# Edge sums of a graph attention layer: one-hot blocks made four at a time on VectorE, five of eight heads scaled on ScalarE, eight row slots

## The reference

```python
p = jnp.exp(s - m[src])                                      # one weight per edge and head
denom = jax.ops.segment_sum(p, src, num_segments=n)
alpha = p / jnp.where(denom[src] == 0, 1.0, denom[src])
agg = jax.ops.segment_sum(alpha[:, :, None] * v[dst], src, num_segments=n)
att = agg.reshape(n, C) @ Wo.T + bo
```

## Time and profile before

| | |
|---|---|
| time of the kernel | 6714.76 us median of 3 runs (6714.2 to 6720.42) |
| span of the profiled execution | 6560.1 us |
| median less span (launch and end, outside the trace) | 154.7 us |
| first gather to end of the last add of `attend` | 849.3 to 1169.6 us |
| share of `attend` in the span | 4.9% |
| longest phase, the LSTM (L1654 and others) | from about 1170 us to about 5660 us |

### The profile page before, as it was taken

The page is one execution under the profiler, slowest core; times in us unless marked ns, Lnnn a source line. Parts: engine busy times, 40 slices in busy tenths (PEclk is TensorE's granted clock), DMA queues, the critical chain, the costliest instruction groups (busy, mean ns, idle before and its releaser), DMA issues. The chain is left out here.

```text
span 6560.1 us, 407056 instructions
## 1 busy us (share of the span) xinstructions
PE 5245.2 (80%) x179105; PEld 3616.3 (55%) x179105; DVE 3804.3 (58%) x22336; ACT 1879.1 (29%) x8915; POOL 677.8 (10%) x716
## 2 busy tenths in 40 slices
PE   1989757789777888777887778987777777888999
PEld 1433334566555666556665556665555555554445
DVE  7337857466666666666666666666666666574111
ACT  1210069333333333333333333333333333200100
POOL 0744345000000000000000000000000000252000
PEclk8999979899999999999999999999999999998999
DMA  2235455101000000000000000100000000221110
GB/s 90 77 92 141 117 160 162 59 28 30 1 0 0 17 28 17 0 0 8 27 27 0 0 0 22 30 9 0 0 0 0 0 0 0 77 80 56 68 36 13
DMA packets 172012, 241.50 MB, mean 37 GB/s; under 512 B 90362, under 2 KB 130938, under 8 KB 167827
## 3 DMA queue, kind: packets, MB, share of 16 engines
q0 software_dynamic: 41952, 116.33, 6.5%
q1 hardware_dynamic: 129714, 120.73, 6.0%
HBM read 224.38 MB, written 12.61 MB: 36 GB/s over the span
## 5 line engine op out<-in xcount | busy, mean ns | idle before, releaser
L1654 PE MATMUL l_bank<-l_w,l_hp 128*32 128x128 f16 x160000 | 2486.7, 220 | 823.4 <-DVE l_hp L1942 801.0
L1654 PEld LDWEIGHTS l_bank<-l_w,l_hp 128*32 128x32 f16 x160000 | 2255.6, 97 | 1431.7 <-DVE l_hp L1942 1391.2
L1906 DVE STREAM_TRANSPOSE agg<-l_bank 128x128 f32<-128x128 f32 x2500 | 792.9, 317 | 1176.6 <-PE l_bank L1654 1005.9
L1782 ACT ACTIVATE l_th<-l_z 128x8 f32<-128x8 f32 x2500 | 523.7, 209 | 2153.2 <-DVE l_z L1912 2153.2
L1664 PE MATMUL l_spare<-l_w 128*2 128x512 f16 x12120 | 865.0, 379 | 3.7 <-issue 3.7
L2128 POOL DMA_INDIRECT ga_rows<-r_table,dst_t x176 | 166.9, 948 | 4633.8 <-DMA r_table<-c_r 4508.2
L1787 ACT ACTIVATE l_tc<-l_th 128x2 f32<-128x2 f32 x2500 | 490.5, 196 | 465.5 <-DVE l_th L1929 465.5
L1918 DVE SCALAR_TENSOR_TENSOR l_terms<-l_th 128x4 f32<-128x4 f32 x2500 | 357.0, 143 | 256.7 <-ACT l_th L1782 256.7
L1936 DVE TENSOR_TENSOR l_hp<-l_go,l_tc 128x2 f16<-128x2 f32 x2500 | 422.0, 169 | 132.0 <-ACT l_tc L1787 0.9
L1912 DVE TENSOR_REDUCE l_z<-agg 128x8 f32<-128x24 f32 x2500 | 447.5, 179 | 42.6
L1942 DVE TENSOR_TENSOR l_hp<-l_full,l_hp 128x2 f16<-128x2 f32 x2500 | 422.6, 169 | 43.9 <-DVE l_full L1937 0.6
(11 more groups left out here) (428 smaller groups left out, 4913.8 us busy)
## 6 DMA issues: line engine op xcount, KB each, us to landing
w<-in_g_W SPq DMA_DIRECT2D x128, 128.0 KB, 2.1
w<-in_l_Wx SPq DMA_DIRECT2D x128, 128.0 KB, 2.1
keys<-in_src_by_tile SPq DMA_DIRECT2D x7, 1344.0 KB, 6.8
e_w<-in_e_W SPq DMA_DIRECT2D x2, 4096.0 KB
e_chosen<-chosen SPq DMA_DIRECT2D x24, 256.0 KB, 6.2
wh<-in_l_Wh SPq DMA_DIRECT2D x1, 4096.0 KB, 18.8
late<-in_l_Wh SPq DMA_DIRECT2D x1, 4096.0 KB, 19.0
late<-in_l_Wx SPq DMA_DIRECT2D x1, 4096.0 KB
```

Source lines behind the costliest of these rows:

```text
L1654: mm = pe.matmul(banks[par][q][32 * j:32 * j + 32, 0:128], hp[:, par, k, 30 - 30 * v:62 - 30 * v], w16[:, half, k, j, 256 * q + 128 * v:25 ...
L1782: act.activation(th[:, 2 * q:2 * q + 2, 1:], z[:, q, :].rearrange("p (j m) -> p j m", m=GATES), ACT.Tanh, scale=2.0 ** -Z_BITS).then_inc(s ...
L1906: dve.transpose(turn[:, par, q, :, 1:33], banks[par][q][:, 0:128].rearrange("p (m r) -> p m r", r=32)).then_inc(s_turned[q], 1)
```

## The change

R becomes 8. ON_DVE becomes 3, so VectorE scales heads 0 to 2 (192 elements) and ScalarE five heads. The one-hots of four tiles (AT_ONCE) are made by one comparison of VectorE over 512 elements. There are two such buffers of four. ScalarE makes none. The value load of add(t - 1) moves ahead of scale(t + 1), so it stands directly behind add(t - 2). TensorE sums the weights first and the rows second, and waits for a one-hot buffer only every fourth tile. The accumulator is cleared behind the first comparison, and ScalarE no longer waits for it.

```diff
-    R = 4
-    ON_DVE = 5
+    R = 8
+    ON_DVE = 3
+    AT_ONCE = 4
...
-        onehot, apart = sb("onehot", [P, R, P]), sb("apart", [P, R, P])
-        minus_lo, one = sb("minus_lo", [P, ST]), sb("one", [P, 1])
+        onehot = sb("onehot", [P, 2, AT_ONCE, P])
...
         @block.scalar
         def _(act):
-            act.wait_ge(cleared, 1)
-
-            def mark(t):
-                if t >= R:
-                    act.wait_ge(summed, t - R + 1)
-                act.activation(apart[:, t % R, :], g.numbers_f[:, :], ACT.Square,
-                               bias=minus_lo[:, t:t + 1]).then_inc(squared, 1)
-                act.wait_ge(squared, t + 1)
-                act.activation(onehot[:, t % R, :], apart[:, t % R, :], ACT.Relu, scale=-1.0, bias=one[:, :])
-
-            mark(0)
             for t in range(ST):
-                if t + 1 < ST:
-                    mark(t + 1)
                 i = t % R
...
         @block.vector
         def _(dve):
-            g.link(dve, dve.memset(acc[:, :], 0.0))
-            dve.memset(one[:, :], 1.0)
-            dve.tensor_scalar(minus_lo[:, :], lo[:, :], -1.0, None, ALU.mult).then_inc(cleared, 1)
+            def mark(u):
+                if u >= 2:
+                    dve.wait_ge(summed, AT_ONCE * (u - 1))
+                dve.tensor_tensor(onehot[:, u % 2, :, :], g.numbers_f[:, :].unsqueeze(1).broadcast_to([P, AT_ONCE, P]),
+                                  lo[:, AT_ONCE * u:AT_ONCE * (u + 1)].unsqueeze(2).broadcast_to([P, AT_ONCE, P]),
+                                  ALU.is_equal).then_inc(equal, 1)
...
-            def add(t):
-                node = dve.value_load(tile_node[0:1, t:t + 1], min_val=0, max_val=RT - 1)
+            def node_of(t):
+                return dve.value_load(tile_node[0:1, t:t + 1], min_val=0, max_val=RT - 1)
+
+            def add(t, node):
                 dve.wait_ge(summed, t + 1)
...
+            mark(0)
+            dve.memset(acc[:, :], 0.0).then_inc(cleared, 1)
             scale(0)
             for t in range(ST):
+                node = node_of(t - 1) if t >= 1 else None
                 if t + 1 < ST:
                     scale(t + 1)
+                if t % AT_ONCE == 1 and t + AT_ONCE < ST:
+                    mark(t // AT_ONCE + 1)
                 if t >= 1:
-                    add(t - 1)
-            add(ST - 1)
+                    add(t - 1, node)
+            add(ST - 1, node_of(ST - 1))
...
+                if t % AT_ONCE == 0:
+                    pe.wait_ge(equal, t // AT_ONCE + 1)
                 pe.wait_ge(scaled, t + 1)
-                pe.wait_ge(marked, t + 1)
+                pe.wait_ge(other, t + 1)
                 if t >= 4:
                     pe.wait_ge(added, t - 3)
-                pe.matmul(banks[t % 4][:, 0:C], onehot[:, i, :], rows[:, i, :], start=True, stop=True)
-                pe.matmul(banks[t % 4][:, C:W], onehot[:, i, :], weight[:, t, :], start=True,
-                          stop=True).then_inc(summed, 1)
+                mark = onehot[:, t // AT_ONCE % 2, t % AT_ONCE, :]
+                pe.matmul(banks[t % 4][:, C:W], mark, weight[:, t, :], start=True, stop=True)
+                pe.matmul(banks[t % 4][:, 0:C], mark, rows[:, i, :], start=True, stop=True).then_inc(summed, 1)
```

More of the change, by code:

```diff
@@ L1241, in attend @@
         rows = sb("rows", [P, R, C])
-        onehot, apart = sb("onehot", [P, R, P]), sb("apart", [P, R, P])
-        minus_lo, one = sb("minus_lo", [P, ST]), sb("one", [P, 1])
+        onehot = sb("onehot", [P, 2, AT_ONCE, P])
         banks = [s0.enter_context(nc.psum_tensor(f"at_bank{i}", [P, 1024], F32)) for i in range(4)]
-        passed, cleared, scaled, marked, squared = (sem("passed"), sem("cleared"), sem("scaled"), sem("marked"),
-                                                    sem("squared"))
+        passed, cleared, scaled, equal, other = sem("passed"), sem("cleared"), sem("scaled"), sem("equal"), sem("other")
         summed, added = sem("summed"), sem("added")
@@ L1294, in _ @@
                                          scale=weight[:, t, h:h + 1])
-                ins.then_inc(marked, 1)
+                ins.then_inc(other, 1)
         @block.vector
         def _(dve):
-            g.link(dve, dve.memset(acc[:, :], 0.0))
-            dve.memset(one[:, :], 1.0)
-            dve.tensor_scalar(minus_lo[:, :], lo[:, :], -1.0, None, ALU.mult).then_inc(cleared, 1)
+            def mark(u):
[4 more added lines that the diff above has]
+                                  ALU.is_equal).then_inc(equal, 1)
             def scale(t):
@@ L1316, in add @@
                     dve.wait_ge(added, t)
+                else:
+                    dve.wait_ge(cleared, 1)
                 at = acc[:, bass.ds(node * W, W)]
                 dve.tensor_tensor(at, at, banks[t % 4][:, 0:W], ALU.add).then_inc(added, 1)
+            mark(0)
+            dve.memset(acc[:, :], 0.0).then_inc(cleared, 1)
             scale(0)
             for t in range(ST):
+                node = node_of(t - 1) if t >= 1 else None
                 if t + 1 < ST:
                     scale(t + 1)
+                if t % AT_ONCE == 1 and t + AT_ONCE < ST:
+                    mark(t // AT_ONCE + 1)
                 if t >= 1:
-                    add(t - 1)
-            add(ST - 1)
+                    add(t - 1, node)
+            add(ST - 1, node_of(ST - 1))
         @block.tensor
```

## The result

The changed kernel takes 6685.66 us (median of 4 runs), the kernel before 6717.24 us in the same comparison: a ratio of 0.9952 (95% interval 0.9940 to 0.9964). It is faster by 31.6 us, where 67 were forecast. The predicted 6648 us was 38 us too low. The time lies inside the stated range of 6631 to 6689 us, but the gain is less than half of the forecast one.

The account below looks back on a forecast made before the run. The loop through four slots, 6.48 us or 1.62 a tile, was taken as the bound of `attend`. Gains of 61 (steady part) + 5 (head) - 0.5 + 1.5 (ends) = 67 us gave 6648 us, range 6631 to 6689.

Parts of the forecast that it names:

- the pace: Steady part of `attend`: GpSimd sets 1.27 us a tile, before 1.665; 155 tiles gain 61 us.
- The median is 154.7 us longer than the span of before: Whole kernel: this difference lies around the span and is kept, so the forecast is 6714.8 - 67 = 6648 us.
- The one at 1.44 us a tile: Rival, steady part of `attend`: VectorE sets the pace, 40 us gained, 6675 us; chance 0.17.
- Eight slots: Slot loop of `attend`: at most 0.87 us a tile in place of 1.62, so no longer the bound.
- GpSimd 1.25: Steady part of `attend`: a gather of 0.945 us plus 0.30 between gathers, 1.25 us a tile; the slowest engine.
- VectorE and the block number: VectorE in `attend`: 1.1 to 1.24 us a tile; the block number's load, covered by an add, costs 0 to 0.1.
- load exposed: Rival, VectorE in `attend`: value load waits for the add, 1.65 to 1.75 us a tile, 6710 to 6722 us; chance 0.05.
- GpSimd held off by VectorE: Rival, gathers of `attend`: descriptor building stalls during VectorE's two-operand reads, 1.79 us a tile, 6728 us; chance 0.05.
- DMA keeps the pace: Rival, gathers of `attend`: more in flight only land later, 1.6 us a tile, 10 us gained, 6705 us; chance 0.05.
- Head: Start of `attend` while matrices load: gathers' DMA share fixed, four more tiles fetched early, 5 us gained.
- other 8 us: Head of `attend`: further gain if the gathers' DMA share grew with the number waiting, six more gathers landing.
- Ends: Start and end of `attend`: -0.5 us at the first scaling, +1.5 from last gather to end, 8.8 us becoming 7.

Follow-up runs that it names:

- b0: The kernel before, unchanged, profiled again on a slow chip: 6708.0 us.
- a1: The changed kernel with four slots in place of eight, on a slow chip: 6746.6 us, ratio 1.0049 to the kernel before.
- a2: The changed kernel with the two products in their old order, rows first, on a slow chip: 6680.7 us, ratio 0.9949 to the kernel before.
- a6: The changed kernel with six slots in place of eight, on a quick chip: 6498.9 us, ratio 0.9922 to the kernel before.
- d1: The changed kernel, unchanged, run again on a quick chip: 6491.3 us, ratio 0.9898 to the kernel before.
- e1: The changed kernel without the small product (sums of the weights) from the fifth tile on, on a slow chip: 6696.2 us, one run.

## Why the prediction was wrong, step by step

**The step that failed** is the pace: "GpSimd is the slowest and waits for nobody while slots are free, so its pace is the stage's". Where the two kernels were timed, the pace was 1.52 us and not 1.27. GpSimd and VectorE wait there for sums that are reported late, a wait that the prediction had put at nothing (its own words for it are "hardly any wait of GpSimd for TensorE"). From the thirty-first to the last gather the kernel before takes 241.3 us there (b0) and the changed kernel 222.4. So the term of 61 us for the steady part measured 19.

**The step that hid it** is "The median is 154.7 us longer than the span of before, for what lies around it, and I keep that". In the runs of this record 1.7 to 3.4 us lie around a span. The other 150 us said that the profiled execution and the timed runs were not in the same condition, and that the page did not show the machine on which the change would be timed. It could have been doubted: no row spoke for 155 us of launch, and three timed runs within 6.2 us of each other stood against one span far from all of them. With it the rows were those of a quick chip. In their own condition they did forecast well: 6493 us of span, where the quick chip has 6487.8.

**What that cost.** On slow chips something holds the engines up where a gather would come more often than about every 1.5 us beside full work. The kernel before, at 1.665, lay just above this floor; its `attend` is 318.2 us there and 320.3 on the quick sort. The changed kernel reaches the floor and loses 0.25 us a tile to it: 145 x 0.25 = 36 us, which is the gain that went missing. That the rest came to 31.6 us is owed to the head: it gave 15 us (69.7 to 54.3 us from the first to the thirty-first gather), where 5 were counted. No rival had this mechanism. The one at 1.44 us a tile came closest to the time, 6675 us, but gave the wrong reason: the adds wait for late sums, not VectorE's work, and VectorE is busy 117.00 of 160 us.

**Eight slots** (6.96 / 8 = 0.87 us): the loop ceases to be the bound, right. The loop measured in a1 makes it 7.25 / 8 = 0.91. On slow chips this edit alone brings all of the gain. What the rest is worth on a quick chip, where eight slots with ScalarE's 1.44 us should give less than the 68.5, was not measured.

**GpSimd 1.25**: right. Gathers at 1070.60, 1071.85 and 1073.19 are 1.25 and 1.34 us apart, with 0.30 "issue" ahead, and on the quick chip the stretch has 126 at 1.27, the forecast number. Its waits for TensorE there are 23.7 us in 34 over the whole phase, 8.1 us in 25 of them in the stretch.

**ScalarE 1.20**: right, 627 scalings in 160 us at 0.24 us, 153.19 busy; it is nearly full on the quick chip.

**VectorE and the block number**: right. This is VectorE between two late sums in the changed kernel:

```profile
1069.25 0.69 DVE L1311 TENSOR_TENSOR agg<-agg,at_bank 128x520 f32 x1
1069.86 0.35 DVE L1298 TENSOR_TENSOR at_rows<-at_rows,weight_t 128x192 f32<-128x192 f32 x1
1070.15 0.70 DVE L1311 TENSOR_TENSOR agg<-agg,at_bank 128x520 f32 x1
```

Add to add is 0.90 us, with 0.17 for the comparison 1.07, and 0.29 from scaling to add: the load is covered (the rival "load exposed" wanted 1.65). The scaling takes 0.36 as worked out, the comparison 0.68.

**TensorE 1.08**: right (1071.69 to 1072.77); the order of the products is worth nothing (a2).

**GpSimd held off by VectorE**: wrong. The gather takes 946 ns at the median, 944 before, with comparison and scaling beside it.

**DMA keeps the pace**: wrong on quick chips, where the share is 0.72 (0.75 was forecast) at 1.27.

**Head**: mis-sized. 5 us were counted. On the quick chip the tiles from the thirtieth on give 145 x (1.665 - 1.28) = 56 us and the phase 72.1, so about 16 us come from what is ahead of them and behind them (17 in the head, -1 at the end). The DMA queues (packets, MB, share of 16 engines) in the 20 us that begin 5 us after the first gather, of the kernel before and of the changed kernel:

```profile
q1 hardware_dynamic: 17023, 3.13, 84.4%
q0 software_dynamic: 491, 1.62, 34.3%
```

```profile
q0 software_dynamic: 1186, 3.89, 70.4%
q1 hardware_dynamic: 16816, 0.54, 48.4%
```

The gathers' share doubled while the same 17,000 small packets of the weights went by: there their share was not fixed, it rose with the gathers waiting, and the big loads came later. The prediction had read its fixed share from a later stretch, 870 to 890 us, in which the matrices load. The changed kernel has this in the like stretch, 875 to 895 us, in which some 3000 of the small packets are still to come:

```profile
q1 hardware_dynamic: 3154, 5.53, 72.7%
q0 software_dynamic: 677, 2.21, 32.1%
...
at_rows<-v_table,dst_t POOLq DMA_INDIRECT x10, 14.0
```

The gathers' share rose there only from 23.9% to 32.1%, and they land after 14.0 us in place of 7.3. With six slots (a6) it is 18.0%. So in that stretch more gathers in flight mostly land later, about as the prediction said. It leaned on the Trainium skill, DMA: Bandwidth & Descriptors, section "Queues, rings and completion order", by which each engine goes round between its queues by packet. The measurements agree with its conclusion, in the main, while the matrices load, and not while the weights do. What parts the two stretches was not tested. For the sum, the "other 8 us" of the text were the better choice.

**Ends**: forecast +1.5 us, measured -0.7 on the quick chip. From the last gather to the end it is 9.5 us (1092.9 to 1102.4), where 7 were forecast and 8.8 were before.

**Sum.** 56 + 16 = 72 in the profiles and 68.5 in the medians, against 67 forecast. On a quick chip the total came out right with a steady part 5 us too large and a head and ends some 10 too small. That the errors cancel is luck.

## What to carry to other kernels

Hold the profiled execution against the timed runs before anything else: when the time less the span is far more than the few microseconds that lie around a span, the profile was taken in other conditions, and a phase that the change does not touch says in which. Where a chip of another sort may run the kernel, compare only runs of one chip, and repeat an edit that looks like a gain on the other sort before it is believed. Eight slots alone brought all of the gain on the slow chips. On a quick chip they were never run alone, so what the moved work adds there is not shown; the move of the heads by itself added nothing that shows in the times.

## What the runs showed of the hardware

Chips (or the conditions that they are in) differ by more than this change moves. In the scatter phase TensorE is held up on slow chips as long as GpSimd issues its scatters (the last at 385.0 us). These are stretches of the kernel before on a slow chip, during the scatters and after them:

```profile
275.00:385.00 110.00, 23.86 (x33) 8.90 (x32) 12.10 (x6) 2.71 (x5) 83.92 (x84) 0.61 0.04 4
395.00:480.00 85.00, 77.87 (x187) 36.72 (x188) 0.00 (x0) 20.27 (x31) 0.00 (x0) 0.92 0.11 37
```

33 matmuls in 110 us, then 187 in 85, all of one line, and gaps such as this one, which the trace explains by nothing but "issue":

```profile
295.73 5.08 PE L724 MATMUL st_bank<-st_wq,xn 128*128 128x512 f32 x8 [19.96 <-issue]
```

So in two phases the same holds: GpSimd's indirect transfers beside dense work of TensorE are free on quick chips and cost time on slow chips, some 150 us in one and 36 us in the other. It is not the bandwidth of the DMA engines, of which the scatter phase uses 4%. What is shared there stays open. One trace of it: on slow chips some semaphore events are missing from the records, 44,759 are there in the changed kernel's first profile and 51,338 on the quick chip (d1). Of the 176 `summed` the first has 151, d1 all. The issue line of the gathers gives their time to landing on the quick chip and none in the changed kernel on the slow one:

```profile
at_rows<-v_table,dst_t POOLq DMA_INDIRECT x176, 3.7
```

```profile
at_rows<-v_table,dst_t POOLq DMA_INDIRECT x176
```

and waits of the add are put down to "remote", as none is in d1. A path for the events or the trace records of the engines that is too slow would fit the late `summed`, the missing records and the long register instructions of e1 alike. This is argued and not shown. The Trainium skill, NOTIFIC — the notification-queue block, section "Interfaces", says that this block can hold up the engines that send it records when a buffer of it fills. No run here shows that this is what happens, nor whether a run without a profiler would have it.
